# First layer's table tile stored in four quarters instead of two halves, two of them issued ahead of the xb store, in a four-layer graph network kernel

## The chip, the cores and the metric

The kernel runs on one core of one Trainium2 chip. The metric is device time in microseconds of one execution. The kernel before took 6701.82 us, the median of three runs (6699.92 to 6706.92).

## The reference, cut to what matters

Four graph layers run one after the other on 6250 nodes of 256 features and 100,000 edges. Each layer's result is added to its input and normalised. The change touches only the first layer, whose relation weights are combinations of 8 bases:

```python
weight = jnp.einsum('rb,bio->rio', w_comp, bases)      # 32 relations from 8 bases
xw = jnp.einsum('ni,rio->nro', h, weight)
msg = xw[src, rel_type] * norm
out = jax.ops.segment_sum(msg, dst, num_segments=h.shape[0])
```

## The kernel before, in words

The program goes through phases with a barrier of all engines between them: setup, `layer0`, fused, gat, scores, softmax, sum, last. `layer0` is the phase of the change. It writes `table`, which holds xw, in device memory; the next phase gathers rows of it.

`layer0` works on NW1 = 49 windows of 128 nodes. A window goes through three steps, one iteration of every engine's loop (index k) apart, so that an iteration holds window k in its first step, window m = k - 1 in its second and window q = k - 2 in its third.

- **First step, bases.** PE multiplies the window with the 8 bases: 4 banks of 512 columns, 6 matmuls each (`base_products`, L1363). ACT copies the banks to the tile `l_xb` (`evacuate_xb`, L1177). SP stores this 1 MB in device memory as `xb_dram` (L358), waits until it has landed, and reads it back in another layout into one of three buffers `l_S`, as 8 DMAs of 128 KB in rows of 1 KB (L366). The round trip brings (node, base) pairs onto the partitions.
- **Second step, halves of precision.** ACT rounds `l_S` into `l_S_high` (`high_rows`, L1183) and DVE takes the rest as `l_S_low` (`low_rows`, L761).
- **Third step, combinations.** PE makes 16 banks (TBANKS) of 3 matmuls each (`combine`, L1378), combination i for relations of group i // 4. Even banks are copied by ACT (L1194), odd ones by DVE (L772), into `l_table`, a tile of 32 rows of 256 floats on each partition (4 MB) of which there is one. Copies 0 to 3 fill its first quarter, 0 to 7 its first half. SP stores it in two halves of 2 MB (`store_half`, L349 to L352, the issue is L351), and each half has a semaphore, `l_t_free[h]`. The copies of the next window into a half wait for the landing of that half's store: ACT before copies 0 and 8, DVE before copies 1 and 9.

PSUM has 5 banks for combinations, so PE's combination n waits for copy n - 5, and combination 0 of a window waits for `l_low`.

The order on each engine is written out by hand. SP in iteration k: wait for `l_xb_free` and store xb (L357, L358); half 0 of window q; wait for xb's landing; 8 loads of `l_S`; half 1 of window q. ACT in iteration k: copies 0, 2, xb bank 0, copy 4, xb bank 1, copy 6, xb bank 2, copy 8, xb bank 3, copy 10, `high_rows`, copies 12 and 14. DVE: copies 1, 3, 5, the transposed rows of window k + 1, copies 7, 9, 11, `low_rows`, copies 13 and 15. PE: combinations 0 to 15, with the four sets of base products behind combinations 1, 3, 5 and 7 and two transposes behind combination 2. In the last two iterations there is no first step.

Of the kernel before, what the change touches and what calls it, by code (L numbers as in the profile page):

```python
# [15 lines left out]
D = 256  # L16
# [16 lines left out]
def build(nc, x, edges, dst_last, bases, w_compT, w1, gate1T, w2, w2T, a_src, a_dst, edge_wT,  # L33
# [30 lines left out]
    with ExitStack() as ctx:  # L64
# [9 lines left out]
        def sem(name):  # L74
            return ctx.enter_context(nc.semaphore(name))
# [44 lines left out]
        JS = P // QUADS  # L120
        TBANKS = JS // 2
# [4 lines left out]
        l_table = A[:, 0:JS * D].rearrange("p (j c) -> p j c", c=D)  # L126
# [122 lines left out]
                                           "high", "low", "full", "act", "dve"))  # L249
        l_xb_out = sem("l_xb_out")  # L250
        l_s_in = [sem(f"l_s_in{u}") for u in range(3)]
        l_t_free = [sem(f"l_t_free{h}") for h in range(2)]

        class Walk:

# [50 lines left out]
        def table_place(i):  # L306

            gp, quad = i // 4, i % 4
            return l_table[:, gp * 8:(gp + 1) * 8, :].rearrange("p (g q) c -> p g q c", q=4)[:, :, quad, :]

        def comb_bank(n):

            return ps[:, 3 + n % 5, :]
# [5 lines left out]
        def _(sp):  # L319
# [24 lines left out]
            def layer0_transfers(_):  # L344
                xb_rows = xb_dram.rearrange("(w p) c -> w p c", p=P)
                rows = table.rearrange("(w p) c -> w p c", p=P)

                def store_half(q, h):
                    sp.wait_ge(l_act, TBANKS // 2 * q + TBANKS // 4 * (h + 1))  # L349
                    sp.wait_ge(l_dve, TBANKS // 2 * q + TBANKS // 4 * (h + 1))  # L350
                    sp.dma_start(rows[q, :, h * (JS // 2) * D:(h + 1) * (JS // 2) * D],  # L351
                                 l_table[:, h * (JS // 2):(h + 1) * (JS // 2), :].rearrange("p j c -> p (j c)")).then_inc(l_t_free[h], 16)  # L352

                for k in range(NW1 + 2):
                    q = k - 2
                    if k < NW1:
                        sp.wait_ge(l_xb_free, XBANKS * (k + 1))  # L357
                        sp.dma_start(xb_rows[k], l_xb).then_inc(l_xb_out, 16)  # L358
                    if q >= 0:
                        store_half(q, 0)  # L360
                    if k < NW1:
                        sp.wait_ge(l_xb_out, 16 * (k + 1))
                        if k >= 3:
                            sp.wait_ge(l_full, TBANKS * (k - 2))
                        for g in range(BASES):
                            sp.dma_start(l_S[k % 3][:, g * D:(g + 1) * D],  # L366
                                         xb_dram[k * P + g * 16:k * P + (g + 1) * 16, :].rearrange("i (b o) -> (i b) o", o=D)).then_inc(l_s_in[k % 3], 16)
                    if q >= 0:
                        store_half(q, 1)
                for h in range(2):  # L370
                    sp.wait_ge(l_t_free[h], 16 * NW1)

            def head_loads():
# [188 lines left out]
            def last_stores(wk):  # L562
# [14 lines left out]
                for p in range(NW1):  # L577
                    sp.wait_ge(f_normed, 3 * NW1 + p + 1)
                    sp.dma_start(out[bass.ds(at[p] * P, ROWS), :], last_acc[0:ROWS, bass.ds(at[p], 1), :].squeeze(1)).then_inc(stored, 16)
                    if p + 2 < NW1:  # L580
                        load_x(p + 2)
                sp.dma_start(full[ROWS:P], last_acc[ROWS:P, 0:NW1 - 1, :]).then_inc(stored, 16)
                sp.wait_ge(stored, 16 * NW1 + 16)

            run(sp, {"setup": setup, "layer0": layer0_transfers, "fused": fused_transfers, "gat": gat_transfers, "sum": sum_transfers,
                     "last": last_stores, "scores": spill, "softmax": keep_ex})

# [60 lines left out]
        def _(dve):  # L648
# [93 lines left out]
            def layer0(_):  # L742
                for b in range(XBANKS):
                    bank = slice(b * 512, (b + 1) * 512)
                    dve.wait_ge(l_b_high, b + 1)
                    dve.tensor_tensor(b_low[:, :, bank], raw_bases[:, :, bank], b_high[:, :, bank].bitcast(F32), ALU.subtract).then_inc(l_b_low, 1)
                dve.wait_ge(l_c_high, 1)
                dve.tensor_tensor(comb_low, comb_raw, comb_high.bitcast(F32), ALU.subtract).then_inc(l_c_low, 1)

                def turned_halves(k):  # L750
                    turned = ps[:, 0, 0:D].rearrange("p (c n) -> p c n", c=2)
                    if k >= 2:
                        dve.wait_ge(l_xb_full, XBANKS * (k - 1))
                    dve.wait_ge(l_turned, k + 1)
                    dve.tensor_copy(xt_high[:, k % 2, :, :], turned).then_inc(l_xt_high, 1)
                    dve.wait_ge(l_xt_high, k + 1)
                    dve.tensor_tensor(xt_low[:, k % 2, :, :], turned, xt_high[:, k % 2, :, :].bitcast(F32), ALU.subtract).then_inc(l_xt_ready, 1)

                def low_rows(m):
                    dve.wait_ge(l_high, m + 1)  # L760
                    dve.tensor_tensor(l_S_low[m % 3], l_S[m % 3], l_S_high[m % 2].bitcast(F32), ALU.subtract).then_inc(l_low, 1)  # L761

                turned_halves(0)
                for k in range(NW1 + 2):
                    q, m = k - 2, k - 1
                    for i in range(1, TBANKS, 2):
                        if q >= 0:
                            h, n = i // (TBANKS // 2), TBANKS * q + i
                            if i % (TBANKS // 2) == 1 and q >= 1:
                                dve.wait_ge(l_t_free[h], 16 * q)  # L770
                            dve.wait_ge(l_full, n + 1)
                            dve.tensor_copy(table_place(i), comb_bank(n).rearrange("p (g c) -> p g c", g=2)).then_inc(l_dve, 1)  # L772
                        if i == 5 and k + 1 < NW1:
                            turned_halves(k + 1)
                        if i == 11 and 0 <= m < NW1:
                            low_rows(m)
                dve.wait_ge(l_low, NW1)
# [303 lines left out]
            def attention_sum(_):  # L1081
# [50 lines left out]
                for k in range(NW1 + 1):  # L1132
                    p = k - 1
                    for j in range(SLOT):
# [24 lines left out]
                dve.wait_ge(s_xt_ready, NW1)  # L1159

            run(dve, {"setup": setup, "fused": fused, "layer0": layer0, "gat": gat, "last": last,
                      "scores": scores, "softmax": softmax, "sum": attention_sum})


        @block.scalar
        def _(act):
            def layer0_copies(_):
                for b in range(XBANKS):
                    bank = slice(b * 512, (b + 1) * 512)
                    act.activation(b_high[:, :, bank], raw_bases[:, :, bank], ACT.Copy).then_inc(l_b_high, 1)  # L1170
                act.activation(comb_high, comb_raw, ACT.Copy).then_inc(l_c_high, 1)

                def evacuate_xb(k, b):
                    if b == 0 and k >= 1:
                        act.wait_ge(l_xb_out, 16 * k)
                    act.wait_ge(l_xb_full, XBANKS * k + b + 1)
                    act.activation(l_xb[:, b * 512:(b + 1) * 512], ps[:, 1 + b % 2, :], ACT.Copy).then_inc(l_xb_free, 1)  # L1177

                def high_rows(m):
                    if m >= 2:  # L1180
                        act.wait_ge(l_full, TBANKS * (m - 1))
                    act.wait_ge(l_s_in[m % 3], 16 * BASES * (m // 3 + 1))
                    act.activation(l_S_high[m % 2], l_S[m % 3], ACT.Copy).then_inc(l_high, 1)  # L1183

                act.wait_ge(l_b_low, XBANKS)
                for k in range(NW1 + 2):
                    q, m = k - 2, k - 1
                    for i in range(0, TBANKS, 2):
                        if q >= 0:
                            h, n = i // (TBANKS // 2), TBANKS * q + i  # L1190
                            if i % (TBANKS // 2) == 0 and q >= 1:
                                act.wait_ge(l_t_free[h], 16 * q)
                            act.wait_ge(l_full, n + 1)
                            act.activation(table_place(i), comb_bank(n).rearrange("p (g c) -> p g c", g=2), ACT.Copy).then_inc(l_act, 1)  # L1194
                        if i in (2, 4, 6, 8) and k < NW1:
                            evacuate_xb(k, i // 2 - 1)
                        if i == 10 and 0 <= m < NW1:
                            high_rows(m)
                act.wait_ge(l_act, TBANKS // 2 * NW1)
# [84 lines left out]
            def sum_copies(_):  # L1284
# [19 lines left out]
                for k in range(NW1 + 2):  # L1304
                    p, q = k - 1, k - 2
                    for j in range(SLOT):
# [11 lines left out]
                act.wait_ge(s_bank_free, S_BANKS * NW1)  # L1318

            run(act, {"layer0": layer0_copies, "fused": fused_copies, "last": last_deviations, "gat": gat_copies,  # L1320
                      "scores": scores, "softmax": softmax, "sum": sum_copies})

# [308 lines left out]
```

## Time and profile before

| | |
|---|---|
| median of three runs | 6701.82 us |
| the profiled execution's own time | 6704.29 us |
| its span, first to last instruction | 6702.5 us |
| mean granted TensorE clock | 0.848 |
| PE busy | 5232.6 us (78%) |
| DVE busy | 3958.7 us (59%) |
| POOL busy | 3601.0 us (54%) |
| ACT busy | 1597.0 us (24%) |
| stores of the table's halves, L351 | 98 DMAs of 2048 KB, median 9.4 us to landing |
| stores of xb, L358 | 49 DMAs of 1024 KB, median 3.9 us to landing |

All times of the trace count from the first instruction of the profiled execution. Busy time of PE is that of matmuls, and a matmul is counted until its modelled end, so it overlaps the next. PEclk is the granted share of TensorE's full clock. A line of the timeline such as SP's gives the start of an issue and how long it took the queue to issue it; the data land later. "q" behind an engine is its queue.

### The profile page before, as it was taken

How to read it: one execution, taken by the hardware profiler on the slowest of the kernel's cores; microseconds unless marked ns; L12 is line 12 of the kernel's file. 1: busy time of each engine (PE TensorE's matmuls, PEld its weight loads, DVE VectorE, ACT ScalarE, POOL GpSimd, SP SyncE). 2: the span in 40 equal slices, each digit the busy share in tenths (PEclk: the TensorE clock that was granted, in tenths of full speed). 3: DMA queues.
4: the chain of work that ended last, by engine and by line, in shares of the span. 5: the costliest groups of instructions: out<-in, count | busy, mean ns of one | idle time of the engine just before them, and what ended most of it. 6: DMA issues, size and time to landing. Idle time of an engine off the chain costs nothing.

```text
span 6702.5 us, 77622 instructions
## 1 busy us (share of the span) xinstructions
PE 5232.6 (78%) x19175; PEld 3659.0 (55%) x19176; DVE 3958.7 (59%) x9469; ACT 1597.0 (24%) x3103; POOL 3601.0 (54%) x3549
## 2 busy tenths in 40 slices
PE   5988886999998777777666666519999998777776
PEld 3777774777777433333344444306777876333333
DVE  4444445666664666666666666567766665555555
ACT  2444443444444000000122222212333332000000
POOL 0000003777775777777677777503333333777776
PEclk8999998999999777777788888659999998666666
DMA  5888886666665444444677777416767675444443
GB/s 201 321 315 321 313 321 231 218 215 215 218 214 205 122 124 123 124 124 123 198 241 245 242 244 244 155 57 217 236 235 238 230 241 177 117 116 117 116 116 111
DMA packets 467591, 1330.89 MB, mean 199 GB/s; under 512 B 136962, under 2 KB 261740, under 8 KB 409893
## 3 DMA queue, kind: packets, MB, share of 16 engines
q1 hardware_dynamic: 306773, 883.65, 37.1%
q0 software_dynamic: 160464, 443.17, 23.0%
q8 instruction: 143, 2.34, 0.1%
q14 instruction: 211, 1.73, 0.1%
HBM read 688.06 MB, written 638.42 MB: 198 GB/s over the span
## 4 chain that ended last, share of the span: by engine, by line
PE 54%; DMA 13%; DVE 11%; issue 9%; POOL 5%; SPq 4%; ACT 2%; DVEq 1%; ACTq 0%; POOLq 0%
PE ps L1399 26%; PE ps L1573 10%; PE ps L1423 8%; DMA table<-A 7%; PE ps L1556 5%; DMA work<-place_dram 3%; POOL A L629 2%; POOL ring L629 2%; SPq L366 2%; DVE W L814 2%; DVE A L814 2%; DMA xb_dram<-W 2%; PE ps L1378 1%; SPq L476 1%; PE ps L1363 1%
## 5 line engine op out<-in xcount | busy, mean ns | idle before, releaser
L617 POOL DMA_INDIRECT ring<-table,idx x2490 | 2370.3, 952 | 1908.1 <-DVEq L838 1045.7
L1399 PE MATMUL ps<-ring,W 128*128 128x256 f32 x3320 | 1207.2, 482 | 421.0 <-DVE W L814 260.4
L1399 PEld LDWEIGHTS ps<-ring,W 128*128 128x128 f32 x3320 | 685.7, 230 | 864.0 <-issue 411.9
L814 DVE TENSOR_SCALAR W<-iota,dloc,norm 128x128 f32<-128x128 f32 x1660 | 596.9, 360 | 773.6 <-PE ps L1399 763.4
L1399 PE MATMUL ps<-ring,A 128*128 128x256 f32 x1660 | 722.5, 542 | 273.7 <-DVE A L814 220.1
L642 POOL TENSOR_TENSOR ring<-ring,work 128x1024 f32<-128x1024 f32 x208 | 404.9, 1948 | 878.2 <-DMA ring<-rows_dram 878.2
L1573 PE MATMUL ps<-W_r,work_r 128*128 128x512 f32 x1960 | 701.1, 440 | 0.0
L832 DVE TENSOR_TENSOR X<-X,ps 128x256 f32 x1660 | 685.2, 413 | 13.0 <-PE ps L1399 10.6
L1399 PEld LDWEIGHTS ps<-ring,A 128*128 128x128 f32 x1660 | 341.1, 248 | 621.8 <-DVE A L814 381.2
L1378 PE MATMUL ps<-ring_r,work_r 128*128 128x512 f32 x1568 | 556.8, 407 | 109.1 <-DVE A_r L761 68.8
L1423 PE MATMUL ps<-W_r,work_r 128*128 128x512 f32 x1568 | 560.8, 440 | 0.0
L772 DVE COPY A<-ps 128x512 f32<-128x512 f32 x392 | 261.5, 688 | 480.5 <-DMA table<-A 286.1
L1144 DVE TENSOR_TENSOR X<-X,ps 128x264 f32 x830 | 351.8, 424 | 324.9 <-PE ps L1556 267.7
L1556 PE MATMUL ps<-ring,targets 128*128 128x264 f32 x1660 | 482.6, 396 | 53.9 <-DVE X L1144 23.7
L814 DVE TENSOR_SCALAR A<-iota,dloc,norm 128x128 f32<-128x128 f32 x830 | 295.8, 357 | 376.4 <-PE ps L1399 368.7
L629 POOL DMA_INDIRECT ring<-gat_table,ix x416 | 402.9, 969 | 140.2 <-issue 115.2
L629 POOL DMA_INDIRECT A<-gat_table,ix x416 | 403.3, 970 | 126.9 <-issue 121.7
L1224 ACT ACTIVATE A<-ps,gate 128x256 f32<-128x256 f32 x784 | 329.0, 471 | 549.5 <-PE ps L1423 549.4
L1270 ACT ACTIVATE A<-ps 128x528 f32<-128x528 f32 x416 | 254.2, 611 | 808.0 <-DVE A L975 438.6
L1378 PEld LDWEIGHTS ps<-ring_r,work_r 128*128 128x128 f32 x1568 | 301.9, 193 | 199.4 <-DVE A_r L761 83.1
L1573 PEld LDWEIGHTS ps<-W_r,work_r 128*128 128x128 f32 x1960 | 369.3, 188 | 75.9
L1512 PE MATMUL ps<-W,onehot 128*128 x832 | 299.0, 493 | 120.0 <-DVE A L975 119.5
(239 smaller groups left out, 7267.4 us busy)
## 6 DMA issues: line engine op xcount, KB each, us to landing
table<-A SPq DMA_DIRECT2D x98, 2048.0 KB, 9.4
ring<-rows_dram SPq DMA_DIRECT2D x208, 528.0 KB, 4.6
table<-A SPq DMA_DIRECT2D x98, 1024.0 KB, 4.6
table<-A SPq DMA_DIRECT2D x49, 1280.0 KB, 5.4
table<-W SPq DMA_DIRECT2D x49, 1280.0 KB, 7.0
rows_dram<-ring SPq DMA_DIRECT2D x52, 1056.0 KB, 4.7
rows_dram<-A SPq DMA_DIRECT2D x52, 1056.0 KB, 4.6
xb_dram<-W SPq DMA_DIRECT2D x49, 1024.0 KB, 3.9
```

Of the source, the lines that this page charges most:

```text
L617: pool.indirect_dma_start(out=f_ring[:, s % NR, :], out_offset=None, in_=src, in_offset=bass.IndirectOffsetOnAxis(ap=idx[:, s:s + 1], axis ...
L629: pool.indirect_dma_start(out=place_[:, j, :], out_offset=None, in_=gat_table, in_offset=bass.IndirectOffsetOnAxis(ap=ix[:, h, j:j + 1], a ...
L642: pool.tensor_tensor(rows_, rows_, s_ex[:, c % 4].unsqueeze(3).to_broadcast([P, CH, HEADS, HD]), ALU.mult).then_inc(s_weighed, 1)
L814: return dve.tensor_scalar(marks_[:, k % G, :], iota[:, :], dloc[:, k:k + 1], norm[:, k:k + 1], ALU.is_equal, ALU.mult).then_inc(wk.onehot ...
L832: dve.tensor_tensor(a, a, ps[:, s % banks, 0:D], ALU.add).then_inc(wk.added, 1)
L1144: dve.tensor_tensor(a, a, ps[:, s % SB, 0:GROW], ALU.add).then_inc(s_added, 1)
L1224: ins = act.activation(f_unit[v][:, (b % 4) * 512 + i * D:(b % 4) * 512 + (i + 1) * D], bank[:, i * D:(i + 1) * D], ACT.Copy, scale=gate[: ...
L1378: ins = pe.matmul(comb_bank(n), c[:, quad, :], rows[:, pair], start=(n_ == 0), stop=(n_ == 2))
L1399: pe.matmul(ps[:, s % banks, 0:D], marks_[:, s % G, :], f_ring[:, s % NR, :], start=True, stop=True).then_inc(wk.step_done, 1)
L1423: ins = pe.matmul(ps[:, SB + 1 + b % 4, :], rows[:, q % 2, c, :], w[:, c, b * 512:(b + 1) * 512], start=(n == 0), stop=(n == len(terms) - 1))
L1556: pe.matmul(ps[:, s % SB, 0:GROW], s_marks[:, s % (2 * CH), :], s_rows[c % 4][:, s % CH, :], start=True, stop=True).then_inc(s_done, 1)
L1573: ins = pe.matmul(ps[:, SB + 1 + m % 4, :], rows[:, q % 2, c, :], w[:, c, b * 512:(b + 1) * 512], start=(n == 0), stop=(n == len(terms) - 1))
```

## The change

The tile is stored in four quarters of 1 MB (8 rows on each partition), each with a semaphore of its own. In SP's iteration, quarters 0 and 1 are issued first, ahead of the wait for `l_xb_free` and the store of xb. Quarter 2 stands where half 0 stood, quarter 3 where half 1 stood. ACT and DVE wait before copies 0, 4, 8, 12 and 1, 5, 9, 13.

```diff
-        l_t_free = [sem(f"l_t_free{h}") for h in range(2)]
+        l_t_free = [sem(f"l_t_free{h}") for h in range(4)]
...
-                def store_half(q, h):
-                    sp.wait_ge(l_act, TBANKS // 2 * q + TBANKS // 4 * (h + 1))
-                    sp.wait_ge(l_dve, TBANKS // 2 * q + TBANKS // 4 * (h + 1))
-                    sp.dma_start(rows[q, :, h * (JS // 2) * D:(h + 1) * (JS // 2) * D],
-                                 l_table[:, h * (JS // 2):(h + 1) * (JS // 2), :].rearrange("p j c -> p (j c)")).then_inc(l_t_free[h], 16)
+                def store_quarter(q, h):
+                    sp.wait_ge(l_act, TBANKS // 2 * q + TBANKS // 8 * (h + 1))
+                    sp.wait_ge(l_dve, TBANKS // 2 * q + TBANKS // 8 * (h + 1))
+                    sp.dma_start(rows[q, :, h * (JS // 4) * D:(h + 1) * (JS // 4) * D],
+                                 l_table[:, h * (JS // 4):(h + 1) * (JS // 4), :].rearrange("p j c -> p (j c)")).then_inc(l_t_free[h], 16)
 
                 for k in range(NW1 + 2):
                     q = k - 2
+                    if q >= 0:
+                        store_quarter(q, 0)
+                        store_quarter(q, 1)
                     if k < NW1:
                         sp.wait_ge(l_xb_free, XBANKS * (k + 1))
                         sp.dma_start(xb_rows[k], l_xb).then_inc(l_xb_out, 16)
                     if q >= 0:
-                        store_half(q, 0)
+                        store_quarter(q, 2)
                     if k < NW1:
...
                     if q >= 0:
-                        store_half(q, 1)
-                for h in range(2):
+                        store_quarter(q, 3)
+                for h in range(4):
                     sp.wait_ge(l_t_free[h], 16 * NW1)
...
-                            h, n = i // (TBANKS // 2), TBANKS * q + i
-                            if i % (TBANKS // 2) == 1 and q >= 1:
+                            h, n = i // (TBANKS // 4), TBANKS * q + i
+                            if i % (TBANKS // 4) == 1 and q >= 1:
                                 dve.wait_ge(l_t_free[h], 16 * q)
...
-                            h, n = i // (TBANKS // 2), TBANKS * q + i
-                            if i % (TBANKS // 2) == 0 and q >= 1:
+                            h, n = i // (TBANKS // 4), TBANKS * q + i
+                            if i % (TBANKS // 4) == 0 and q >= 1:
                                 act.wait_ge(l_t_free[h], 16 * q)
```

## Rows read from the trace of the kernel before

**Rows 1.** The page's span, and its DMA line of 40 slices (167.6 us each)

```profile
span 6702.5 us, 77622 instructions
...
DMA  5888886666665444444677777416767675444443
```

**Rows 2.** Stretches: busy PE, PEld, DVE, ACT, POOL, then PEclk, DMA share, GB/s

```profile
122.67:1032.86 910.19, 813.47 (x3409) 646.16 (x3408) 381.28 (x506) 372.30 (x599) 0.00 (x0) 0.97 0.84 319
1032.86:1075.95 43.09, 28.57 (x108) 21.47 (x106) 17.01 (x21) 13.94 (x21) 0.00 (x0) 0.90 0.85 341
```

**Rows 3.** Chain of work that ended last, 398 to 425 us (start, us, what)

```profile
398.71 0.32 ACT A L1194
...
399.20 0.59 ACT W L1177
...
400.25 9.54 DMA table<-A
...
410.81 7.81 DMA table<-A
...
419.76 3.90 DMA xb_dram<-W
```

**Rows 4.** Timeline of SP's queue, same stretch (start, us until issued)

```profile
399.82 0.33 SPq L358 DMA_DIRECT2D xb_dram<-W  x1
...
403.73 6.99 SPq L366 DMA_DIRECT2D A<-xb_dram  x8
410.81 0.38 SPq L351 DMA_DIRECT2D table<-A  x1
```

**Rows 5.** Timeline of DVE, same stretch

```profile
395.60 0.69 DVE L772 COPY A<-ps 128x512 f32<-128x512 f32 x1 [1.25 <-PE ps L1378]
...
399.68 0.69 DVE L772 COPY A<-ps 128x512 f32<-128x512 f32 x1 [0.28 <-PE ps L1378]
...
404.33 1.28 DVE L772 COPY A<-ps 128x512 f32<-128x512 f32 x2
```

**Rows 6.** Waits of the first layer, longest in total

```profile
ACT A L1194 <- DMA table<-A: 427.9, 86, 6.8
```

**Rows 7.** Same columns, three windows from combination 0 to combination 0

```profile
404.47:424.48 20.01, 18.62 (x74) 14.76 (x74) 8.40 (x12) 8.18 (x13) 0.00 (x0) 0.91 0.84 320
424.48:444.86 20.38, 17.34 (x75) 13.54 (x75) 8.20 (x12) 8.01 (x13) 0.00 (x0) 1.00 0.80 306
444.86:464.72 19.86, 18.44 (x74) 14.76 (x74) 8.39 (x12) 8.21 (x13) 0.00 (x0) 0.91 0.85 323
```

**Rows 8.** Timeline of PE where three windows begin

```profile
404.47 0.50 PE L1378 MATMUL ps<-ring_r,work_r 128*128 128x512 f32 x1 [2.10 <-DVE A_r L761]
...
424.48 0.50 PE L1378 MATMUL ps<-ring_r,work_r 128*128 128x512 f32 x1 [1.39 <-DVE A_r L761]
...
444.86 0.50 PE L1378 MATMUL ps<-ring_r,work_r 128*128 128x512 f32 x1 [2.77 <-DVE W_r L761]
```

**Rows 9.** Timelines of ACT and DVE in a window that PE held up

```profile
458.64 0.60 ACT L1194 ACTIVATE A<-ps 128x512 f32<-128x512 f32 x1 [1.69 <-PE ps L1378]
...
460.43 1.91 ACT L1183 ACTIVATE ring_r<-A 128x2048 fp32r<-128x2048 f32 x1
...
462.38 2.29 DVE L761 TENSOR_TENSOR A_r<-A,ring_r 128x2048 fp32r<-128x2048 f32 x1 [1.06 <-ACT ring_r L1183]
```

**Rows 10.** L358 to landing, then how long one issue of L366 takes

```profile
DMA to landing us min/median/max: 3.9/3.9/4.3
...
L366 SPq DMA_DIRECT2D A<-xb_dram x248: 332/497/1513, 146.8 to 1042.2; - x124
```

**Rows 11.** Chain of work that ended last, end of the layer

```profile
1042.78 9.55 DMA table<-A
...
1057.61 11.28 PE ps L1378 x48
...
1069.68 6.27 DMA table<-A
```

## The prediction

> **What bounds the kernel now.** I read the page first. The first layer ends at 1076 us of the 6702.5, and in its slices the DMA engines are busy to eight tenths [rows 1]. Only this layer is touched, so only it is costed. The stretches show it: 46 periods take 910.19 us, 19.79 us each, with a DMA share of 0.84, PE busy 813 us and a mean granted clock of 0.97. The layer's end takes another 43.09 us [rows 2]. So nothing is full, and I look for a loop of waits.
>
> The longest wait is ACT's for the landing of table stores: 427.9 us, 86 times [rows 6], that is 8.7 us per window. The chain shows which landing. A store of half 1, issued at 410.81, lands after 7.81 us; only then may ACT make copy 8, and xb bank 3 stands behind it (398.71, 399.20). Then xb can be stored, 3.9 us to landing; the eight loads of `l_S` are issued, 6.99 us; and behind them in SP's queue stands the next half 1 at 410.81 [rows 3, 4]. Sum: 7.8 + 1.1 + 3.9 + 7.0 + 0.2 = 20.0 us, one period. The loop is one of order. DVE's copy 7 ended at 396.29, so half 0 was ready then and went out at 400.25, 4.0 us late, behind xb. Copy 15 ended at 405.61, and half 1 went out at 410.81, 5.2 us late, behind the loads [rows 3, 4, 5]. The landing that gates copy 8 is that of a store that stands behind the loads.
>
> **The change part by part.** *Copy 8's gate.* It is now quarter 2, which goes out ahead of the loads. The loop above is cut: the 7.0 us of issuing no longer stand between two landings that gate xb. What is late next is PE with the two conversions at the window's end. From copy 8 to `high_rows` are 1.79 us and to `low_rows` 3.74 us, when PE and not a landing held copy 8 up; `low_rows` takes 2.29 us, and then PE may begin the next window [rows 9]. PE reaches copy 8 after 9 combinations, 4 sets of base products and the transposes. A bank of 3 matmuls takes 11.28 / 16 = 0.70 us [rows 11]; I take 0.68, the pace without that stretch's pauses, and 1.36 for a set of six, with 0.2 for the transposes and 0.25 until the copy starts: 6.1 + 5.4 + 0.45 = 12.0 us. The period is then 12.0 + 3.74 + 2.29 = 18.1 us. A second way gives the same: windows at whose end PE waited only 1.4 us are those in which PE was the bound. The one from 404.47 took 20.01 us at a clock of 0.91 and ended with an idle time of 1.39 us [rows 7, 8]. Half a clock for 3.4 us costs 1.7 us (0.09 of 20.01 is 1.8), so at full clock it takes 18.3. I take 18.3.
>
> *Do the transfers fit?* Zero is combination 0. By the paces above, copy 3 is done at 5.2, copy 7 at 10.7, xb is ready at 13.1, copy 11 at 14.7 and copy 15 at 19.3. A transfer of 1 MB lands 3.9 us after its issue [rows 10]; a second MB costs 6.27 - 3.9 = 2.4 us more [rows 11]. A quarter has the shape of the xb store (8 KB on each of 128 partitions), so its price is 3.9 alone and 2.4 behind another. Quarter 0 lands at 9.1, quarter 1 at 14.6. xb stands behind quarter 1 and lands at 17.0, as it would alone. Quarter 2 lands at 19.4. The loads are issued from 17.0 to 24.0 and have landed by 27.9 (one of 128 KB takes no longer than a whole MB). Quarter 3 goes out at 24.1, behind the loads as half 1 did, and lands by 29.6. The next quarter 0 is ready at 23.5 and goes out at 24.5, 1.0 us late, as SP is still in the loads. The wants are: xb's tile at 21.3 (landed 17.0), copy 4 at 24.9 (quarter 1, 14.6), copy 8 at 30.3 (quarter 2, 19.4), `high_rows` at 32.1 (loads, 27.9), copy 12 at 33.8 (quarter 3, 29.6), and copy 0 of the next window at 37.5 (quarter 0, about 31). The smallest slack is 4.2 us. That is the cover of everything I cost at nothing: SP's two further issues of 0.38 us, the waits added on ACT and DVE before copies 4, 5, 12 and 13, and xb behind two stores in the queue. If the cover went, xb late by x would hold PE's base products, and quarter 3 late by x would hold copies 12 to 15.
>
> *Steady gain:* 46 x (19.79 - 18.3) = 68.5 us.
>
> *The end of the layer.* There PE has only combinations, and the stores of 2 MB are the bound: one waits 9.55 us, the last 6.27 [rows 11]. From the last xb store the changed kernel needs 5.2 us to the next combination 0, 12.5 for window 47 (copy 10 at 7.7, then 0.5 + 1.95 + 2.29), 11.3 for window 48, 0.7 for the last copy and 3.9 for a last quarter: 33.6 us. The transfers alone (xb 3.9, loads and 10 quarters at 2.4 per MB) need 30.3, and some us more for holes while loads are issued. Between 33.6 and these I take 35, so 43.1 - 35 = 8 us saved.
>
> *The clock.* At half clock a window costs 1.7 us more. It fell in windows that began after PE had stood idle 2.10 and 2.77 us (0.91), and not in the one after 1.39 us (1.00) [rows 7, 8]. In the new state every window should begin after some 1.4 to 1.6 us. I leave two falls in, 3.4 us back.
>
> **Sum:** 68.5 + 8 - 3.4 = 73 us. The profiled execution's own time is 6704.3, 2.5 above the median of 6701.8. That makes 6631 for it and **6629** for the median, 1.1% less.
>
> **The rivals.**
>
> *A. The clock keeps falling as now.* The mean of 0.97 over 910 us is 27 us, 0.6 per window. For it: PE is then the bound, so a fall can no longer hide in another wait. Against: the falls came after idle times that should be gone. Period 18.9, gain 41 + 8 = 49: 6653.
>
> *B. A loop through the DMA queue takes over.* From xb's landing: loads 6.0 to 7.0, quarter 3 3.9, then quarters 0, 1 and xb at 2.4: 17.1 to 18.1, under 18.3. But the same half store takes 7.81 us once and up to 9.55 elsewhere [rows 3, 11], so up to 1.7 us may be added: 18.8 to 19.8. Only one store covers the loads' issue now, where half 0 had two MB. At 19.2: 27 + 8 = 35, 6667.
>
> *C. It does not do what it says,* because the landings are late for want of bandwidth and not of order. For it: DMA share 0.84. Against: half 0 and half 1 were each ready 4 to 5 us before their issue. Then about 6700.
>
> *D. Slower, by the queue.* xb now waits behind quarters 0 and 1, and the path of quarter 3 becomes a loop over two windows: its landing frees copy 12, from there to the xb store two windows on are 15.9 us (18.3 + 13.1 - 15.5), xb 3.9 + 2 x 2.4, loads 7.0, quarter 3 9.5. The sum is 41.1, 20.55 per window, 0.76 more than now: 46 x 0.76 - 8 = 27 us slower, 6729. It decides as soon as xb, loads and quarter 3 together take over 2 x 19.79 - 15.9 = 23.7 us. By the rows above they take 16.5 at most, since quarter 0 has long landed when xb goes out. The Trainium skill (DMA: Bandwidth & Descriptors, section "Bandwidth") speaks for this rival: it wants DMAs of 1 MiB or more and has 6.15 us for 1 MB against 79 for 16 MB, so that smaller pieces each pay a fixed part. By its figure five such transfers one behind another would be 30.8 us a window, more than a period. The trace does not agree: xb takes 3.9 us, and the store issued 0.4 us behind it at 400.25 does not wait for it.
>
> **How the numbers follow.** Forecast 0.60, A 0.17, B 0.13, C 0.04, D 0.06. The low end is a period of 18.1 with no falls: 46 x 1.69 + 9 = 87, 6615. The high end takes in A and the middle of B: 6668. Outside are C, D and half of B. A measurement of this kernel can tell about 0.2%, 13 us. Forecast, A and B are all faster by more than that: 0.90. C is 0.04. D is 0.06.
>
> **What would show it.** Periods from xb store to xb store of 18.1 to 18.5 us; ACT's waits for the table's DMAs fall from 428 us to near none; PE idles some 1.5 us before each window for `low_rows`, and the granted clock in the layer is 0.99 or more; the layer's end takes 34 to 36 us. Copies 8 still starting right at a landing would make it wrong (B or D, told apart by which quarter), and so would a clock of 0.97 at periods near 18.9 (A). The other phases should keep their times within some us.

## The result and the profile after

The changed kernel takes 6630.43 us, the median of four runs (6626.24 to 6634.45), against 6702.83 for the kernel before, the median of four (6699.92 to 6706.92; the table of the profile before has the first three). The ratio is 0.9891, with a 95% interval of 0.9874 to 0.9909: 72 us less. Its profiled execution took 6634.45 us, with a span of 6632.7.

The page after, span and DMA line:

```profile
span 6632.7 us, 78011 instructions
...
DMA  5888885666665444444777777426767775434443
```

The two stretches that answer to [rows 2], cut at the same events (third store of xb, last store of xb, last landing of the table). The columns are those of [rows 2].

```profile
124.37:970.59 846.22, 781.78 (x3404) 626.01 (x3403) 385.40 (x505) 382.87 (x598) 0.00 (x0) 1.00 0.89 343
970.59:1005.45 34.86, 26.04 (x112) 20.50 (x110) 17.63 (x22) 14.65 (x21) 0.00 (x0) 0.99 0.92 370
```

46 periods take 846.22 us, 18.40 each, where they took 19.79 [rows 2]; the layer's end takes 34.86 us instead of 43.09. The granted clock is 1.00 over the 46 periods. A single fall could hide in that rounding, so each of the 46 was also read by itself: none is under 1.00. In the kernel before, 17 of the 46 are (0.83 to 0.91). The ledger between the two spans: 64.0 us from the periods, 8.2 from the end, -1.7 because the third store of xb came at 124.37 us instead of 122.67, -0.7 in all that follows the layer (5626.55 us before, 5627.25 after). That is 69.8, the difference of the spans.

The chain of work that ended last, one window long, which answers to [rows 3]:

```profile
419.53 1.92 ACT ring_r L1186
...
421.48 2.31 DVE W_r L764
...
423.83 1.65 PE ps L1381 x6
...
435.29 2.06 PE ps L1381 x9
...
437.86 1.92 ACT ring_r L1186
```

There is no transfer in it. The chain goes from `high_rows` on ACT to `low_rows` on DVE, to PE's first combination, and through PE's matmuls (all but the first and last row of them left out) to the next `high_rows`, 18.33 us later. The waits of the first layer, which answer to [rows 6], and the start of a window, which answers to [rows 8], say the same:

```profile
ACT A L1197 <- PE ps L1381: 490.3, 296, 4.1
...
PE ps L1381 <- DVE A_r L764: 49.8, 33, 4.8
...
ACT A L1197 <- DMA table<-A: 0.2, 1, 0.2
```

```profile
405.37 0.50 PE L1381 MATMUL ps<-ring_r,work_r 128*128 128x512 f32 x1 [1.39 <-DVE A_r L764]
```

ACT waited 427.9 us for the landings of table stores; now it waits 0.2 us for them and 490.3 us for PE. PE idles 1.39 us before this window and 1.38 to 1.42 before the others, for `low_rows`.

SP's queue, which answers to [rows 4] (quarters 0 and 1 of the next window are counted with quarter 3 in the last row):

```profile
418.83 0.33 SPq L361 DMA_DIRECT2D xb_dram<-W  x1
420.49 0.33 SPq L351 DMA_DIRECT2D table<-A  x1
422.74 4.35 SPq L369 DMA_DIRECT2D A<-xb_dram  x8
427.19 7.88 SPq L351 DMA_DIRECT2D table<-A  x3
```

xb goes out at 418.83, quarter 2 at 420.49, the loads take 4.35 us to issue where they took 6.99 in [rows 4] (means over the windows: 4.5 and 6.05), and quarter 3 goes out at 427.19. The end of the layer, which answers to [rows 11]:

```profile
975.58 7.79 PE ps L1381 x33
...
988.18 11.28 PE ps L1381 x48
...
999.48 0.70 DVE A L775
...
1000.25 5.21 DMA table<-A
```

### The profile page after: what moved, and what is told of

It is laid out like the page before. It is cut to its first block, busy times and chain, and to the rows that moved or that the text cites. A ratio compares the mean times of both kernels' runs of the same rounds, so it can differ in the third digit from the quotient of the medians.

```text
span 6632.7 us, 78011 instructions
## 1 busy us (share of the span) xinstructions
PE 5188.2 (78%) x19175; PEld 3635.0 (55%) x19176; DVE 3942.1 (59%) x9469; ACT 1607.2 (24%) x3103; POOL 3607.1 (54%) x3549
## 4 chain that ended last, share of the span: by engine, by line
PE 63%; DVE 12%; issue 10%; POOL 6%; DMA 5%; ACT 2%; SPq 2%; DVEq 1%; POOLq 0%; ACTq 0%
PE ps L1402 26%; PE ps L1576 10%; PE ps L1426 8%; PE ps L1381 6%; PE ps L1559 5%; PE ps L1366 4%; POOL A L632 3%; POOL ring L632 3%; DMA work<-place_dram 2%; DVE W L817 2%; DVE A L817 2%; ACT ring_r L1186 1%; SPq L479 1%; DVE A_r L764 1%; DMA A<-gat_table,ix 1%
## 5 line engine op out<-in xcount | busy, mean ns | idle before, releaser
L1381 PE MATMUL ps<-ring_r,work_r 128*128 128x512 f32 x1568 | 540.4, 397 | 72.1 <-DVE A_r L764 49.8
L1559 PEld LDWEIGHTS ps<-ring,targets 128*128 128x128 f32 x1660 | 308.2, 192 | 141.6 <-DVE work_r L1129 31.6
```

The source lines that it names most:

```text
L1381: ins = pe.matmul(comb_bank(n), c[:, quad, :], rows[:, pair], start=(n_ == 0), stop=(n_ == 2))
L1559: pe.matmul(ps[:, s % SB, 0:GROW], s_marks[:, s % (2 * CH), :], s_rows[c % 4][:, s % CH, :], start=True, stop=True).then_inc(s_done, 1)
```

## The experiments

Eleven kernels ran in three groups, each group on a chip of its own. On two of these chips the phases behind the first layer, which gather rows from device memory, are slower (6460 to 6500 us instead of 5627), and the kernel before takes 7574.8 us (first group, e1 to e4) and 7550.91 us (third group, e7, e10 and e11). In the second group (e5, e6, e8, e9) it takes 6706.12 us. The first layer is the same on all: the changed kernel, e1, e7 and e9, the last three of which ran on three chips, have equal periods in it to 0.02 us. For the kernel before, whose loop is another bound, there is no trace from these chips; its period of 19.79 is carried over from the one trace that there is. The ratios are taken against the kernel before on the same chip, and the readings from the layer's rows. Where a period is given, it is the time between the third and the last store of xb, over 46. The fence of each run has this stretch; where a second row stands, it is the end of the layer, and its right edge is the last landing of the table. The columns are those of [rows 2]. Means and medians of issues and landings are over the windows of the periods. In all of them the line numbers are a few off those of the listing.

**e1, the split alone.** From the changed kernel:

```diff
-                    if q >= 0:
-                        store_quarter(q, 0)
-                        store_quarter(q, 1)
                     if k < NW1:
...
                     if q >= 0:
-                        store_quarter(q, 2)
+                        store_quarter(q, 0)
+                        store_quarter(q, 1)
...
                     if q >= 0:
+                        store_quarter(q, 2)
                         store_quarter(q, 3)
```

> The changed kernel with the quarters and their four semaphores kept, but no quarter ahead of xb: SP issues xb, quarters 0 and 1, the loads, quarters 2 and 3. Copy 8 waits for quarter 2, which again stands behind the loads, but is 1 MB where half 1 was 2. Theory (a loop of order, and PE the bound once it is under 18.4 us): landing 7.8 - 2.4 = 5.4 (up to 7), 1.1, xb 3.9, loads 6.1 to 7.0, 0.2 makes 16.7 to 19.2, mostly under PE's 18.4, so periods of 18.4 to 18.8 and 6630 to 6655 us: the split alone brings most of the gain. Rival 1 (it is the place in the queue, ahead of the reorder, that counts): periods stay at 19.8 and the time at 6700. Rival 2 (bandwidth): 6700 as well.

```profile
125.28:971.63 846.35, 781.48 (x3404) 626.09 (x3403) 385.54 (x505) 382.79 (x598) 0.00 (x0) 1.00 0.91 343
971.63:1010.32 38.69, 27.70 (x112) 21.43 (x110) 17.54 (x22) 14.41 (x21) 0.00 (x0) 0.94 0.95 380
```

Measured: 7504.0 us, ratio 0.9904 (0.9887 to 0.9922). The period is 18.40 us, the clock 1.00, to the hundredth that of the changed kernel. ACT still waits 137 us in the periods for landings of table stores, 2.9 us a window, but PE isn't held up by it. The place ahead of xb is not needed for the periods here; it brings 3.8 us, once, at the end of the layer (38.69 against 34.86).

**e2, the move alone.** From the kernel before:

```diff
+                    if q >= 0:
+                        store_half(q, 0)
                     if k < NW1:
                         sp.wait_ge(l_xb_free, XBANKS * (k + 1))
                         sp.dma_start(xb_rows[k], l_xb).then_inc(l_xb_out, 16)
-                    if q >= 0:
-                        store_half(q, 0)
```

> The kernel before with half 0 issued ahead of xb, still in halves of 2 MB. Theory: half 1 now waits behind loads that have no store ahead of them (issue 3.9 to 4.4 instead of 6 to 7), but xb stands behind 2 MB (6.3 - 2.4 left + 2.4 = 6.3 to landing instead of 3.9): 6.3 to 7.8 for half 1, 1.1, 6.3, 4.2, 0.2 makes 18.1 to 19.6. Periods 18.6 to 19.4, 6645 to 6690 us: a part of the gain, smaller than the split's. Rival (the move is what counts): 18.4 and 6630. Rival (only the split counts): 19.8 and 6700.

```profile
124.26:1000.60 876.34, 796.31 (x3412) 636.35 (x3411) 385.78 (x506) 379.89 (x599) 0.00 (x0) 0.98 0.84 331
```

Measured: 7537.88 us, ratio 0.9958 (0.9944 to 0.9972). The period is 19.05 us: half of the steady gain. On the mean of its windows the loads take 3.9 us to issue (2.1 less than in the kernel before) and xb takes 6.45 us to land (2.5 more), the two sizes of the expectation. These two alone would make the loop longer. What tips it is the third part: half 1 lands 7.26 us after its issue, where it took 8.46 in the kernel before (1.2 less). The three add up to 0.8 us less, and the period is 0.74 shorter.

**e3 and e4, twice as many loads.** In the kernel before and in the changed one:

```diff
-                        for g in range(BASES):
-                            sp.dma_start(l_S[k % 3][:, g * D:(g + 1) * D],
-                                         xb_dram[k * P + g * 16:k * P + (g + 1) * 16, :].rearrange(...)).then_inc(...)
+                        for g in range(2 * BASES):
+                            sp.dma_start(l_S[k % 3][g % 2 * 64:(g % 2 + 1) * 64, g // 2 * D:(g // 2 + 1) * D],
+                                         xb_dram[k * P + g * 8:k * P + (g + 1) * 8, :].rearrange(...)).then_inc(...)
```

> The kernel before with each load of 128 KB cut in two of 64 KB, so SP issues 16 for a window instead of 8. Bytes and row length stay. Theory (the issue of the loads lies in the loop that sets the period): the issue grows by some 3 us a window, and each window by the same: 46 x 3 = 140 us, 6840 (6780 to 6890). Rival (the landings are late for want of bandwidth): 6700 to 6715.

```profile
129.47:1226.56 1097.09, 876.08 (x3412) 678.42 (x3411) 379.27 (x506) 373.77 (x599) 0.00 (x0) 0.91 0.69 264
```

Measured: 7767.66 us, ratio 1.0253 (1.0236 to 1.027), 193 us more. The period is 23.85, 4.1 us more. An added load cost twice what I took: 16 are issued in 12.0 us on the mean, where 8 took 6.05, because a load on 64 partitions takes 0.60 us to issue and one on 128 takes 0.43 when nothing holds it up (e11 has both). The chain of this run is the loop of [rows 3] with the longer issue in it (of the 16 issues one row stands):

```profile
599.78 6.55 DMA table<-A
...
606.85 0.60 ACT W L1177
607.47 3.88 DMA xb_dram<-W
...
617.28 0.60 SPq L366
...
623.61 6.50 DMA table<-A
```

The theory's sign and mechanism hold, but the time is just over the upper end of what I gave (190 us more), and the period grew by 4.1 us and the issue by 5.9. The landing of half 1 gives the rest back: on the mean it lands 6.7 us after its issue here, 8.46 in the kernel before. My reading is that when half 1 goes out later, less is left in the queue ahead of it.

> The changed kernel with the same 16 loads. Theory (PE and the two conversions are the bound, and quarter 3, which stands behind the loads, has some 4 to 7 us to spare before copy 12 wants its place): the added 3 us are hidden, periods stay at 18.4, 6626 to 6640 us. Rival B of the prediction (a loop through the queue just under PE's period, 17.1 to 18.1): it would now be 20 to 21, 6700 to 6750.

```profile
128.72:1172.66 1043.94, 872.09 (x3419) 692.70 (x3417) 386.42 (x506) 395.11 (x600) 0.00 (x0) 0.89 0.72 276
```

Measured: 7717.24 us, ratio 1.0189 (1.0172 to 1.0206). A miss: I expected 18.4 and got 22.69. With 10.5 us for the issue of the loads, a loop that the changed kernel has room for becomes the bound. The timeline of SP's queue shows it:

```profile
612.13 10.42 SPq L369 DMA_DIRECT2D W<-xb_dram  x16
622.64 1.90 SPq L351 DMA_DIRECT2D table<-A  x3
624.60 1.25 SPq L361 DMA_DIRECT2D xb_dram<-W  x1
625.93 1.20 SPq L351 DMA_DIRECT2D table<-A  x1
634.31 11.05 SPq L369 DMA_DIRECT2D A<-xb_dram  x16
```

From the first load at 612.13 SP waits for nothing until xb is out: the loads, three quarters, xb at 624.60. xb then stands behind quarters 3, 0 and 1, lands 9.7 us after its issue, and the next loads begin at 634.31. That is rival B of the prediction, at 22.2 us. With the changed kernel's 4.5 us of issue it would be 16.2, an estimate from this window; from the means of all windows (period 22.69, issue 10.5) it is 16.7. Both leave the landing of xb as it is here, and no run shows that loop at its own length.

**e8 and e9, two more loads.** A cost that should show in one kernel and not in the other: only the first two loads are cut in two.

```diff
-                        for g in range(BASES):
+                        for g in range(BASES + 2):
+                            if g < 4:
+                                sp.dma_start(l_S[k % 3][g % 2 * 64:(g % 2 + 1) * 64, g // 2 * D:(g // 2 + 1) * D],
...
+                            else:
+                                sp.dma_start(l_S[k % 3][:, (g - 2) * D:(g - 1) * D],
...
```

> The kernel before with only two of its eight loads cut in two, 10 issues. By the run with 16 loads an added issue costs 0.65 to 0.75 us. Theory (the issue lies in the loop that sets the period): 1.0 to 1.5 us more a window, 45 to 70 us more than the kernel before. Rival (hidden): within 10 us.

```profile
124.75:1044.57 919.82, 814.69 (x3410) 646.60 (x3409) 381.05 (x506) 374.59 (x599) 0.00 (x0) 0.96 0.82 315
```

Measured: 6717.13 us, ratio 1.0016 (1.0007 to 1.0026), 11 us more; the period is 20.00, 0.21 more. A miss: the issue grew by 1.2 us on the mean (7.24 against 6.05), and the period by a sixth of that. Half 1 lands 7.5 us after its issue, on the mean, where it took 8.46 in the kernel before, so it gives 0.96 us back. What is left is 0.23 us, and the period has grown by 0.21. So of the time from xb's landing to half 1's issue, the last microsecond was nearly free: during it the queue worked off what stood ahead of half 1.

> The changed kernel with the same 10 loads. Theory, as the run with 16 loads left it: there is a loop through the queue (loads, issues of quarters 3, 0, 1 and xb, landing of xb behind them) of 16.2 us, with 2.2 us of room under PE's 18.4. The added 1.3 to 1.5 us are hidden: periods stay at 18.4 and the layer ends at 1003 to 1010 us, 65 to 75 us under the kernel before. Rival (there is no room, every added issue counts as in the kernel before): periods of 19.7 to 19.9, a gain of 10 us or less.

```profile
124.51:970.73 846.22, 781.80 (x3404) 626.08 (x3403) 385.41 (x505) 382.88 (x598) 0.00 (x0) 1.00 0.88 343
```

Measured: 6634.53 us, ratio 0.9888 (0.9871 to 0.9904). The period is 18.40, that of the changed kernel, though the loads take 5.8 us to issue. The issue grew by 1.3 us and the period by nothing, so the room under PE's period is at least that. The estimates of 16.2 and 16.7 agree with it.

**e7, order alone, in halves.** From the kernel before, half 1 ahead of the loads:

```diff
                     if q >= 0:
                         store_half(q, 0)
+                        store_half(q, 1)
...
-                    if q >= 0:
-                        store_half(q, 1)
```

> The kernel before, still in halves of 2 MB, with half 1 issued ahead of the loads instead of behind them: xb, half 0, half 1, loads. SP now waits for copy 15 before it issues the loads. Theory (the period before was set by half 1 standing last in the queue, so that xb's store could not follow until all else had drained): half 1 is ready at 19.3 us after combination 0, goes out then, lands behind half 0 by 26.6 and is wanted at 30.3; the loads land by 30 and are wanted at 32.1. Periods of 18.4 to 18.8, the layer ends at 1010 to 1030 us, 45 to 65 us under the kernel before. Rival (the size of the stores is what counts): periods of 19.5 and more, within 15 us of the kernel before.

```profile
123.09:969.97 846.88, 781.80 (x3404) 625.85 (x3403) 383.85 (x505) 378.09 (x598) 0.00 (x0) 1.00 0.90 342
969.97:1013.17 43.20, 28.23 (x112) 21.48 (x110) 17.45 (x22) 14.30 (x21) 0.00 (x0) 0.93 0.84 341
```

Measured: 7479.13 us, ratio 0.9911 (0.9894 to 0.9927). The period is 18.41 us. No quarter and no new semaphore, and the whole steady gain is there. ACT still waits 242 us for landings of table stores, and PE is the bound all the same; what counts is whether PE is held up. Its end stays at 43.2 us, that of the kernel before (43.09): none of the 8.2 us there comes from this order.

**e5 and e6, the two conversions moved up.** If PE and the conversions bound the changed kernel but not the one before, taking them off the window's end must help one and not the other.

```diff
-                        if i == 10 and 0 <= m < NW1:
+                        if i == 6 and 0 <= m < NW1:
                             high_rows(m)
...
-                        if i == 11 and 0 <= m < NW1:
+                        if i == 7 and 0 <= m < NW1:
                             low_rows(m)
```

> The kernel before with the two conversions moved up: ACT rounds the loaded rows behind copy 6 and xb bank 2 instead of behind copy 10, DVE takes the rest behind copy 7 instead of behind copy 11. Nothing is left out. Theory (in the kernel before the loop of order sets the period, and PE only in windows after a fall of the clock): the loop half 1, copy 8, xb, loads is untouched, so periods stay at 19.2 to 19.8 and the gain on the kernel before of the same chip is 0 to 25 us. Rival (PE and the conversions were the bound there too): periods fall by 1.4 us, 60 us or more.

```profile
123.69:1032.02 908.33, 823.55 (x3404) 638.79 (x3403) 378.27 (x505) 376.97 (x598) 0.00 (x0) 0.97 0.84 319
```

Measured: 6704.87 us, ratio 0.9993 (0.9984 to 1.0003), no change. The period is 19.75.

> The changed kernel with the same move of the two conversions. Theory (PE and the conversions at the window's end are its bound): the 1.39 us in which PE idles ahead of each window go, and the period is what PE's matmuls need, 74 at 0.227 us and some, 16.9 to 17.1 us, unless the loop through the queue (loads 4.5, four issues 1.6, four transfers 10.1: 16.2) comes in. The layer ends some 60 to 70 us earlier than in the changed kernel, at 935 to 945 us, and the gain on the kernel before is 130 to 140 us. Rival (landings or bandwidth are its bound): periods stay at 18.0 to 18.4.

```profile
122.58:896.63 774.05, 772.76 (x3403) 627.11 (x3403) 381.01 (x505) 390.06 (x598) 0.00 (x0) 1.00 0.96 374
896.63:935.09 38.46, 28.77 (x112) 22.44 (x110) 16.84 (x22) 12.94 (x20) 0.00 (x0) 0.90 0.89 359
```

Measured: 6560.13 us, ratio 0.9778 (0.9762 to 0.9794), 146 us under the kernel before. It is faster than both kernels. The period is 16.83 us, just under what I gave, and the layer ends at 935.09. Its chain is PE alone, from one window into the next without a pause (30 matmuls are the ten combinations across the border):

```profile
506.47 6.90 PE ps L1381 x30
513.37 1.39 PE ps L1366 x6
...
523.28 6.96 PE ps L1381 x30
```

The DMA engines carry the same bytes in 15% less time than in the kernel before, at a share of 0.96 and 374 GB/s. That rules out rival C: at 0.84 and 319 [rows 2] bandwidth was not what made the landings late.

**e10 and e11, what stands behind e6.** e10 is e1 with the conversions moved up, e11 is e9 with them moved up; the edits are those shown.

> The kernel with quarters but none ahead of xb (xb, quarters 0 and 1, loads, quarters 2 and 3), and with the two conversions moved up as before. It asks whether the place ahead of xb is worth anything once PE leaves room. Theory: the loop quarter 2 (5.6 us to landing behind the loads), 1.1, xb 3.9, loads 6.2, 0.2 is 17.0 us and just above PE's 16.8; periods of 17.0 to 17.6, the layer ends at 945 to 975 us, 10 to 35 us above the same kernel with two quarters ahead (935 us). Rival (the place is worth nothing but the layer's end): periods of 16.8 and an end at 939.

```profile
124.57:918.14 793.57, 781.11 (x3411) 627.51 (x3411) 381.15 (x505) 386.78 (x599) 0.00 (x0) 1.00 0.97 365
```

Measured: 7432.89 us, ratio 0.9842 (0.9826 to 0.9859). The period is 17.25 and the layer ends at 956.8. Both lie in the ranges given. With PE out of the way the place ahead of xb is worth 0.42 us a window. The loop is in the chain: xb is stored, the loads are issued (left out between the first two rows), quarter 2 goes out behind them and lands, then come copy 8, xb bank 3 and the next xb:

```profile
503.72 3.92 DMA xb_dram<-W
...
513.75 6.74 DMA table<-A
520.51 0.60 ACT A L1196
521.11 0.50 ACT W L1179
521.62 3.90 DMA xb_dram<-W
```

> The changed kernel with the conversions moved up and the 10 loads. Theory of the loop through the queue (loads 5.7, four issues 1.6, four transfers 10.1: 17.4): it is now above PE's 16.8, so periods go to 17.1 to 17.6 and the layer ends 12 to 35 us later than with 8 loads (935 us). Rival (there is no such loop near, SP's waits for ACT ahead of xb, 2.1 us a window, take it up): periods of 16.8 to 16.9, the end at 935 to 941 us.

```profile
125.06:955.87 830.81, 785.10 (x3405) 626.88 (x3405) 381.17 (x505) 385.56 (x599) 0.00 (x0) 1.00 0.89 348
```

Measured: 7468.65 us, ratio 0.9898 (0.9882 to 0.9915). The period is 18.06, 0.5 us over the upper end of what I gave. The chain shows another loop than the one I had named:

```profile
522.87 6.24 DMA xb_dram<-W
...
534.54 2.52 DMA A<-xb_dram
...
537.15 1.23 ACT ring_r L1190
...
540.06 6.87 DMA xb_dram<-W
```

xb lands after 6.24 us, the ten loads are issued, the last lands at 537.06, and `high_rows`, which now stands ahead of copy 8 and xb bank 3 on ACT, has waited for it. Then xb can go out again, 17.2 us after the last time. This window is a short one; the same loop takes 17.4 and 18.5 us in the two that follow (xb issued at 557.45 and 575.94), as the landings vary. Over all periods PE's own matmuls hold about two fifths of the chain, so the 18.06 is not that loop alone. e6 has little of it: ACT waited 1.6 us for the loads in all its periods together.

## Why the prediction was right, point by point

**The bound before.** The loop half 1, copy 8, xb bank 3, xb, loads, half 1 was the bound: e7 cuts it by order alone and e1 by size alone, and both give 18.40 us; e5 leaves it and takes the conversions out of PE's way, and nothing moves. What was wrong is two of its terms, and that they hit 20.0 together is in part luck. The prediction took both from one window, in which the issue of the loads was long (7.0 us; the mean is 6.05) and the landing of half 1 short (7.8; the mean is 8.46). They are not independent: the later half 1 goes out, the sooner it lands after that. e8 puts 1.2 us into the issue and gets 0.96 back from the landing, e3 puts 5.9 in and gets 1.8 back; the periods grow by the rest to within 0.15 us (0.21 and 4.1). So the loads' issue was a part of the loop, but an added microsecond of it cost only a fifth (e8) to two thirds (e3) of a microsecond, and my expectation for e8 missed by that.

**What is late next.** PE with the two conversions, 18.3 us predicted and 18.40 measured, with the idle time of 1.39 us before each window as forecast (1.4 to 1.6). The tenth of a microsecond is 4.5 us of the total. e6 shows that this was the bound: without the idle time the period is 16.83.

**Do the transfers fit.** Yes, with more room than I gave. Quarter 3 of the window shown was issued at 427.19 and landed at 432.70, and copy 12 wanted its place at 439.67: 7.0 us to spare where I had 4.2, because the loads took 4.35 us to issue behind 1 MB instead of the 7.0 I kept from the state behind 2 MB. xb landed in 3.9 us (median of 46), as alone. But the smallest slack against a due time is not the room in the period. e4 showed that: its 6 us of added issue were under the 7.0 of slack, and the period grew by 4.3 all the same. What repeats is the loop through SP's queue, rival B's. I had 17.1 to 18.1 us for it; the estimates from e4 are 16.2 to 16.7, some 2 us under PE's period, and e9 shows 1.3 of them. I also had quarter 0 going out 1.0 us late, with SP still in the loads; in the window that begins at 405.37 SP is done with them at 408.73 and quarter 0 goes out as soon as copy 3 is made, at 410.8.

**The end of the layer.** 35 predicted, 34.86 measured. By e1 and e7, 4.4 of the 8.2 us come from the smaller stores (43.1 to 38.7) and 3.8 from the quarters ahead of xb.

**The clock.** I left two falls in (3.4 us), and there was none. e1, e7 and e9, with the same period, have none either (1.00), and of the kernels of the old loop the one before, e5 and e8 stand at 0.96 to 0.97 and e3 at 0.91.

**The sum.** 73 us predicted; 69.8 between the profiled executions and 72 between the medians. 4.5 too much from the period and 3.4 too little from the clock nearly cancel, which is luck, and the start of the layer and what follows it took 2.4.

**The rivals.** A: no fall was left. B: real as a loop, but under PE's period; it ruled with e4's 6 us of extra issue. C: out by e6. D, slower by the queue: xb landed in its 3.9 us, since quarter 0 had long landed. The figure of the Trainium skill that I set beside it (DMA: Bandwidth & Descriptors, section "Bandwidth"), 6.15 us for 1 MB, was measured on loads issued from GpSimd and does not describe these stores: 3.9 us alone, and quarters in a row follow one another at a share of 0.92 and 370 GB/s in the layer's end. One reading beside it was wrong, though: the half issued at 400.25 behind xb was held up. It took 9.54 us to land [rows 3], where the last one of the layer, alone, takes 6.27 [rows 11]; how much of that is xb ahead of it and how much the loads behind it no run separates.

**What the change does that it need not.** For the periods, one way to bring the landing that gates copy 8 forward is enough: splitting the store (e1), or taking the whole half ahead of the loads (e7). Moving the first stores ahead of xb (e2) gives half. The change, which does all of it, gives no more in the steady state than each of the first two, because PE takes over at 18.40.

## What to carry to other kernels

In a queue served in order, look for the transfer whose landing frees the buffer that the head of the queue is waiting for: it must not stand last. Issue it earlier or make it smaller; here either was enough, and once the next engine is the bound more of it buys nothing. Then look at what that engine idles for: here two conversions placed by habit behind the last copies cost 1.57 us of every window, and moving them up was worth as much again as the change (e6), which it was not while the loop through the queue ruled (e5).

## What the runs showed of the hardware that I had not expected

- How long SP takes to issue a load depends on what stands in the queue. The eight loads took 3.9 us on the mean with no store just ahead (e2), 4.5 behind a quarter of 1 MB, 6.05 behind a half of 2 MB and 7.9 behind both halves (e7).
- A load on 64 partitions takes longer to issue, 0.60 us, than one on 128, 0.43 us, for half the bytes (both in e11, where the loads come in both forms). Here cutting a load by partitions cost issue time twice: more issues, and each a longer one. What makes it longer no run shows; the side in device memory changed with it (8 nodes instead of 16).
- PE stood idle about 1.4 us (1.38 to 1.42) before every one of these windows and the granted clock stayed at 1.00, the upper of its two levels (2.4 GHz). In the kernel before, in the windows that began after 2.10 and 2.77 us of idle time, it was 0.91 on the mean [rows 7], with a stretch at 0.50 (1.2 GHz), read from 405.00 to 408.40 us.
- The DMA engines held 374 GB/s at a share of 0.96 for 774 us, stores to device memory being five sixths of it (e6).
- The chips differ by 15% in what follows the first layer (5627 us against 6460 to 6500), and by nothing that shows in the periods of the first layer at PE's bound (to 0.02 us). That the gathers are the part that differs is not shown.
